# An audio tower's third group moved forward, and the experts' second layer in three 16-bit products

## What is computed

```
interp  = cubic_interpolate_1d(x, 4x);  windows of 64
kw      = 0.5*(w+1.3)^2 + 0.5*exp(-0.5*(w-0.7)^2)
M       = |fft(kw)|;  tok = softmin(M*sigmoid(M-0.12*max), 0.9*max)
x1      = layernorm(tok)
attn    = sigmoid(q k^T * 8) v, 8 heads;  h = tok + relu(attn @ Wo)
x2      = layernorm(h)
shared  = relu(relu(x2 @ sW1) @ sW2) @ sW3
experts = relu(relu(x2 @ eW1[e]) @ eW2[e]) @ eW3[e],  e = 0..3
gated   = the two experts with the largest gates, weighed
out     = h + shared + gated
```

## Time and profile before

| what | us |
|---|---|
| three runs, median (lowest, highest) | 170.97 (167.11, 171.64) |
| profiled execution, its own time | 166.02 |
| its span | 164.2 |
| TensorE matmul busy | 151.4 (92%) |
| ScalarE busy | 113.2 (69%) |
| VectorE busy | 108.6 (66%) |
| GpSimd busy | 54.5 (33%) |

### The profile page before, as it was taken

How to read it: one execution, slowest core, us unless ns; L and a number is a source line. 1 busy time by engine, 2 the same in 40 slices (tenths; PEclk the granted TensorE clock), 3 DMA queues, 4 the chain that set the end, 5 groups by cost and what they waited for, 6 DMA issues and landing times.

```text
span 164.2 us, 6647 instructions
## 1 busy us (share of the span) xinstructions
PE 151.4 (92%) x2824; PEld 91.4 (56%) x2824; DVE 108.6 (66%) x277; ACT 113.2 (69%) x155; POOL 54.5 (33%) x101
## 2 busy tenths in 40 slices
PE   7998695999979999999899999999999999999970
PEld 2488533545446576666657454634756665676760
DVE  2497998989766767776583949776469775454421
ACT  3598972978859898989695989467444827548310
POOL 4000019685896673645235171717000000000000
PEclk9999569999999999999999999999999999999999
DMA  4380000174796676747576000000010100101101
GB/s 110 99 251 0 4 0 0 64 188 112 174 233 197 188 217 173 213 128 227 160 218 173 13 4 4 4 0 0 4 33 4 33 19 16 35 4 31 34 21 43
DMA packets 13182, 14.09 MB, mean 86 GB/s; under 512 B 1241, under 2 KB 12413, under 8 KB 13089
## 3 DMA queue, kind: packets, MB, share of 16 engines
q1 hardware_dynamic: 12864, 13.47, 29.6%
q10 hardware_dynamic: 288, 0.20, 0.4%
HBM read 9.06 MB, written 4.60 MB: 83 GB/s over the span
## 4 chain that ended last, share of the span: by engine, by line
PE 69%; DVE 10%; ACT 7%; DMA 5%; POOL 4%; issue 2%; DVEq 0%; POOLq 0%; ACTq 0%
PE ps L456 14%; PE ps L438 12%; PE ps L558 8%; PE ps L576 7%; PE ps L615 7%; PE ps L467 4%; PE ps L585 3%; DMA y_stage<-YP 3%; DMA YS<-y_stage 2%; PE ps L600 2%; PE ps L317 2%; PE ps L306 2%; PE ps L479 1%; PE ps L492 1%; POOL norm L1262 1%
## 5 line engine op out<-in xcount | busy, mean ns | idle before, releaser
L1169 ACT ACTIVATE probs<-ps 125x1000 f32<-125x1000 f32 x64 | 61.9, 1008 | 11.1 <-PE ps L438 8.7
L456 PE MATMUL ps<-probs,xn 124*32 124x250 f32 (+1 forms) x512 | 39.2, 376 | 0.0
L438 PE MATMUL ps<-YS,XT 128*32 128x500 f16 x448 | 34.2, 376 | 1.6 <-DMA YS<-y_stage 1.5
L456 PEld LDWEIGHTS ps<-probs,xn 124*32 124x32 f32 (+1 forms) x512 | 15.7, 109 | 12.5 <-issue 2.4
L1196 ACT ACTIVATE H2r<-ps,wf 128x500 f32<-128x500 f32 x16 | 10.8, 676 | 15.4 <-PE ps L576 15.4
L838 DVE COPY ZS<-ps 128x250 f32<-128x250 f32 x32 | 12.9, 412 | 9.9 <-PE ps L456 9.8
L1042 DVE TENSOR_TENSOR area<-H2r,ps 128x500 f32<-128x500 f32 x16 | 10.8, 673 | 10.1 <-ACT H2r L1196 8.6
L576 PE MATMUL ps<-area,wf 128*64 128x500 f32 x64 | 16.7, 585 | 0.0
L1183 ACT ACTIVATE area<-ps,wf 128x500 f32<-128x500 f32 x24 | 15.9, 672 | 0.9 <-PE ps L558 0.9
L438 PEld LDWEIGHTS ps<-YS,XT 128*32 128x32 f16 x448 | 10.7, 96 | 9.9 <-ACT probs L1169 4.0
L819 DVE CAST YP<-ps 128x500 f16<-128x500 f32 x14 | 9.5, 677 | 8.5 <-PE ps L397 8.5
(11 more groups left out here) (157 smaller groups left out, 258.2 us busy)
## 6 DMA issues: line engine op xcount, KB each, us to landing
YS<-y_stage SPq DMA_DIRECT2D x40, 125.0 KB, 3.1
y_stage<-YP SPq DMA_DIRECT2D x10, 250.0 KB, 2.8
YS<-y_stage SPq DMA_DIRECT2D x8, 250.0 KB, 3.9
y_stage<-YP SPq DMA_DIRECT2D x8, 125.0 KB, 4.1
tower_out<-res SPq DMA_DIRECT2D x8, 124.0 KB
wf<-wf_in SPq DMA_DIRECT2D x1, 648.0 KB, 5.9
wa<-wa_in SPq DMA_DIRECT2D x1, 512.0 KB, 5.1
ch<-ch_in SPq DMA_DIRECT2D x1, 160.0 KB, 4.9
```

The source lines that it names most:

```text
L438: last = mm(ps[k0:k1, 2 * (n % 2) + j, 0:TG].rearrange("p (h n) -> p h n", h=2), XT[:, g % 3, (2 * bb + cj) * P + k0:(2 * bb + cj) * P + k ...
L456: last = mm(ps[R * hh:R * hh + R, 4 + bb, half * TB:(half + 1) * TB], xn[0:keys, 4 * g + 2 * bb + cj, :], probs[0:keys, n % 3, hh, :], sta ...
L1169: fn(probs[:, n % 3].rearrange("p (j h) n -> p j (h n)", j=2), ps[0:P, 2 * (n % 2):2 * (n % 2) + 2, 0:TG], ACT.Sigmoid, scale=SCORE_SCALE) ...
```

## The change

**Third group a step sooner.** TensorE does x_transpose(2) at step 4 and y_project(2,·) at steps 5 and 6, each one step earlier, with the transpose in bank 6 in place of 7. VectorE does total and variance of `third` before part_low(4), takes x_take(2) before the total of `later`, y_take(2,0) before z_take(0,1), and centre(later) after y_take(2,1). GpSimd computes the token of `later` after the square of `third`. SyncE sends group 2's first half before it reads back group 1's second.

**The second layer of experts.** For groups 1 to 7, layer2(g,0) and layer2(g,1) are three 16-bit products: high weight x high activation, low weight x high, high weight x low. Group 0 keeps the 32-bit product. GpSimd splits the weights into w2p. ScalarE now does relu1 for all four experts. The high part is a cast, `high1(g,e)`, on VectorE; for expert 3 of groups 1 to 4 on ScalarE. The low part is a subtraction on GpSimd, `low1(g,e)`, in order of g and e, behind norm2(7) in its program. H1 now has one buffer, and relu1(g,e) waits for low1 of the group before; the parts lie in H1p, over YS, with two buffers.

The diff, cut to its core:

```diff
+        def high_on_act(g, e):
+            return e == E - 1 and g <= NG // 2
...
-            for k in range(2):
-                send(1, k)
-                read_back(1, k)
+            send(1, 0)
+            read_back(1, 0)
+            send(1, 1)
             send(2, 0)
+            read_back(1, 1)
             send(2, 1)
             read_back(2, 0)
...
-                if n == 5:
+                if n == 4:
                     x_transpose(2)
-                if n in (6, 7):
-                    y_project(2, n - 6)
+                if n in (5, 6):
+                    y_project(2, n - 5)
...
             y_take(1, 0)
-            part_low(4)
             dve.wait_ge(square_pool, 1)
             total(third, masked)
             variance(third)
+            part_low(4)
...
             y_rest(1, 1)
+            x_take(2)
             dve.wait_ge(token_pool, 1)
             total(later, tok)
+            y_take(2, 0)
+            z_take(0, 1)
+            y_take(2, 1)
             centre(later)
-            x_take(2)
-            z_take(0, 1)
-            y_take(2, 0)
-            y_take(2, 1)
             z_take(0, 2)
...
+                    if g == 1 and k == 0:
+                        pe.wait_ge(w2_split, 2)
+                    pe.wait_ge(h1_lo, E * (g - 1) + 2 * k + 2)
+                    for i, (w, h) in enumerate(((0, 0), (1, 0), (0, 1))):
+                        for j in range(2):
+                            e = 2 * k + j
+                            last = mm(ps[F * j:F * j + F, 3 + k, 0:TG], w2p[:, w, e * F:(e + 1) * F],
+                                      H1p[:, g % 2, h, e, :], start=(i == 0), stop=(i == 2))
...
+            def high1(g, e):
+                if high_on_act(g, e):
+                    return
+                dve.wait_ge(l1_act, E * g + e + 1)
+                if g >= 3:
+                    dve.wait_ge(l2_mm, 3 * (g - 2) + e // 2 + 1)
+                v.tensor_copy(H1p[:, g % 2, 0, e, :], H1[:, e, :]).then_inc(h1_hi, 1)
...
                 if g < NG:
                     weigh(g, 0)
+                if g + 1 < NG:
+                    high1(g + 1, 0)
...
                 if g + 1 < NG:
-                    relu1(g + 1, 3)
+                    high1(g + 1, 2)
+                    high1(g + 1, 3)
...
+                if g == 1:
+                    act.wait_ge(l2_mm, e // 2 + 1)
                 if g >= 2:
-                    act.wait_ge(l2_mm, 3 * (g - 1))
+                    act.wait_ge(h1_lo, E * (g - 2) + e + 1)
...
                     if g + 1 < NG:
                         relu1(g + 1, k)
+                    if g + 1 < NG and k == 2:
+                        relu1(g + 1, 3)
+                        if high_on_act(g + 1, 3):
+                            high1(g + 1, 3)
...
             norm2(NG - 1)
+
+            def low1(g, e):
+                if high_on_act(g, e):
+                    pool.wait_ge(h1_hi_act, g)
+                else:
+                    pool.wait_ge(h1_hi, high_count(g, e))
+                if g >= 3:
+                    pool.wait_ge(l2_mm, 3 * (g - 2) + e // 2 + 1)
+                v.tensor_tensor(H1p[:, g % 2, 1, e, :], H1[:, e, :], H1p[:, g % 2, 0, e, :],
+                                ALU.subtract).then_inc(h1_lo, 1)
+
+            for g in range(1, NG):
+                for e in range(E):
+                    low1(g, e)
```

More of the change, by code:

```diff
@@ L222, in build, with high_count, x_bank @@
         unit_of = [(bb, half) for half in range(2) for bb in range(2)]
+        def high_on_act(g, e):
+            return e == E - 1 and g <= NG // 2
+        def high_count(g, e):
+            return sum(1 for n in range(1, g + 1) for i in range(E if n < g else e + 1) if not high_on_act(n, i))
+        def x_bank(g):
+            return {0: 1, 2: 6}.get(g, 7)
         def y_bank(g, k):
@@ L375, in x_transpose @@
                     pe.wait_ge(x2t_cp, g - 4)
-                xt = half_bank(7 if g else 1, 128, 4)
+                xt = half_bank(x_bank(g), 128, 4)
                 for i in range(4):
@@ L570, in layer2 @@
                 if k < 2:
-                    pe.wait_ge(l1_act, 3 * g + (2, 3)[k])
-                    if k == 1:
-                        pe.wait_ge(l1_dve, 2 * g + 1)
-                    for j in range(2):
-                        e = 2 * k + j
-                        last = mm(ps[F * j:F * j + F, 3 + k, 0:TG],
-                                  wf[:, WF["w2"][0] + e * F:WF["w2"][0] + (e + 1) * F], H1[:, g % 2, e, :],
-                                  start=True, stop=True)
+                    if g == 0:
+                        pe.wait_ge(l1_act, 2 * k + 2)
+                        for j in range(2):
+                            e = 2 * k + j
+                            last = mm(ps[F * j:F * j + F, 3 + k, 0:TG],
+                                      wf[:, WF["w2"][0] + e * F:WF["w2"][0] + (e + 1) * F], H1[:, e, :],
+                                      start=True, stop=True)
+                        last.then_inc(l2_mm, 1)
+                        return
[3 more added lines that the diff above has]
+                    for i, (w, h) in enumerate(((0, 0), (1, 0), (0, 1))):
+                        for j in range(2):
+                            e = 2 * k + j
+                            last = mm(ps[F * j:F * j + F, 3 + k, 0:TG], w2p[:, w, e * F:(e + 1) * F],
+                                      H1p[:, g % 2, h, e, :], start=(i == 0), stop=(i == 2))
                 else:
                     pe.wait_ge(l2_act, 3 * g + 2)
-                    pe.wait_ge(l1_dve, 2 * g + 2)
+                    pe.wait_ge(l1_dve, g + 1)
                     for m in range(2):
@@ L1025, in _, with relu_shared @@
             gate_rows(0)
-            def relu1(g, e):
-                n = (E + 1) * g + e
+            def relu_shared(g):
+                n = (E + 1) * g + E
                 dve.wait_ge(l1_mm, n + 1)
@@ L1050, in finish @@
                                 h2[:, 4 * g:4 * g + 4, :], ALU.add).then_inc(res_done, 1)
-            for e in range(3, E + 1):
-                relu1(0, e)
+            relu_shared(0)
             routing_take(0)
@@ L1068, in _ @@
                     weigh(g, 1)
+                if g + 1 < NG:
+                    high1(g + 1, 1)
                 if g == 0:
@@ L1084, in _ @@
                 if g + 1 < NG:
-                    relu1(g + 1, 4)
+                    relu_shared(g + 1)
                 if g == 2:
@@ L1197, in relu2 @@
                    bias=wf[:, WF["b2"][0] + k:WF["b2"][0] + k + 1]).then_inc(l2_act, 1)
-            for e in range(3):
+            for e in range(E):
                 relu1(0, e)
@@ L1286, in _ @@
             square_rows(third)
+            pool.wait_ge(act1, 6)
+            v.tensor_tensor(tok[:, later, 0:NBIN], masked[:, later, :], dist[:, later, :],
+                            ALU.subtract).then_inc(token_pool, 1)
             inverse_deviation(slice(8, 12), third)
```

46 lines of the change are left out of this document (27 added, 19 removed).

## The result

The changed kernel takes 184.28 us (median of 6 runs, 182.73 to 184.88), the kernel before, in the same session, 166.10 (median of 6, 164.62 to 171.64). The ratio is 1.117, with a 95% interval of 1.111 to 1.122. Each ratio here leaves out executions that a disturbed clock set apart, so it can differ a little from the ratio of the medians. The change makes the kernel 18.2 us slower, where +9.7 was forecast. The direction was right and the time lies in the range, but the size was about half of what came.

A forecast was written before the change was run, and what follows sets the result against it. TensorE's queue was taken to bound a group of the last stage. Terms of 6.0 + 1.5 + 2.0 + 0.2 gave +9.7 us on a middle of 169.04, so 178.7 us (+5.7%), range 170.5 to 187.

The forecast's parts named there:

- The main wait: TensorE before layer2(1,0): waits for two GpSimd subtractions behind norm2(7), starting at about 117.8 instead of 111.84, +6.0 us.
- term 3: Feed-forward groups: a new chain of relu, cast and subtractions outweighs TensorE's shorter 16-bit matmuls, +2.0 us in sum.
- term 4: The head: the scores' DMA wait goes, but later VectorE and GpSimd work delays projections, net +0.2 us.
- Term 1: Start of layer2(1,0): it now waits for GpSimd's low1(1,0) and low1(1,1) behind norm2(7), +6.0 us (bounds 4.5 and 7).
- Term 2: After the wait before layer2(1,0): TensorE's clock falls to half speed for some 6 us, +1.5 us (bounds 0 and 3).
- the cast waits for the subtraction: Groups 5 to 7: expert 3's cast on VectorE waits until low1(g,2) ends, +1.4 us more, 180.1 us; chance 0.15.
- The 0.5 for `part_low(4)`: Head: total(third) ahead of part_low(4) on VectorE, for which y_part(5) waits, makes the scores lose 0.5 us.
- The other two waits: Head: y_project(3,0) waits for x_take(3), 0.8 us more than the 0.5; y_project(4,1) is about 0.65 us late.

The follow-up runs named there:

- e3_first2: The changed kernel with group 1's second layer in 32 bits too, so that the split begins with group 2: 177.71 us, ratio 1.078.
- e5_stub_sub: The kernel before with 28 GpSimd subtractions of 128x500 added, into a buffer nobody reads and that nobody waits for: 172.95 us, ratio 1.046.

## Why the prediction was half right

The main wait and its cause came as forecast. What failed is term 3 and, far less, term 4: without group 1 they were put at 1.65 + 0.2 = +1.85 and came out at 11.5. That the time of 184.28 still lies in the range is in part luck. The range was laid around a middle of 169.04 for the kernel before, which then measured 166.10. Counted as a loss, its upper end is 187 - 169.04 = +18.0, and +18.2 came.

- **Term 1, +6.0: right.** 5.8 was measured by the starts, 5.88 by the wait, 6.0 by leaving it out (14.89 to 8.85 in `e3_first2`). The chain came as worked out: the subtraction 1.14 (forecast 1.15), the cast 0.40 (0.41).
- **Term 2, +1.5: the mechanism right, a bit large.** The clock fell. Group 1, which holds this term and the +0.35 of term 3, lost 0.97 in all. It came back after some 3 us of work, not 6. What the term lacked is the second fall, behind the gate's wait; it is part of group 4's loss below.
- **Term 3, +2.0: this is the step that failed.** Of it 0.35 was for group 1, so +1.65 for the others, and these measured about 10.1: group 2 +0.63 (forecast 0), group 3 +5.86 (+0.3), group 4 +1.23 (+0.05), groups 5 and 6 +1.30 (+0.6), the end +1.07 (+0.7). The failing sentence is that of group 2, "the gate's matmuls in the queue and its arithmetic on VectorE and ScalarE set its pace in both: 0", and +0.3 for group 3 beside it. The gate's arithmetic does set the pace there, and for that reason nothing that slows it is free. I asked what TensorE would wait for and priced the new work on GpSimd; I didn't ask what GpSimd's reading does to VectorE's own instructions. Group 4's loss, too, comes from there: it is the clock after the gate's wait of 3.68.
- **The rival "the cast waits for the subtraction" came true in its mechanism,** at a chance of 0.15. It said 5.2 us from layer2(g,2) to layer2(g+1,1); it is 165.46 - 160.27 = 5.19. I had it at +1.4 and for the casts of groups 5 to 7 alone. The hold of the two-input instructions in groups 2 and 3 stood in no rival. With this 1.4 and the 3.65 of `e5_stub_sub`, a number that only the runs gave, the forecast would have been near +14.8.
- **Term 4, +0.2: too small.** It measured +1.38 in the profiles of before and after, 2.0 between the means of four and five traces, and +1.5% (2.4 us) with the head alone. The 0.5 for `part_low(4)` became a wait of 1.47, half of it because `total(third)` was itself held (0.89 in place of 0.17) by GpSimd's subtraction, which the change had moved beside it. The other two waits, for `x_take(3)` and for the projections of group 4, came where they were expected, of 1.03 and 0.94.

The row that speaks for the hold was in the trace of before, and I had not looked for it:

```profile
99.77 0.19 DVE L904 TENSOR_TENSOR gt<-gt 125x32 f32<-125x32 f32 x1
99.94 0.61 POOL L1242 TENSOR_TENSOR lnsq<-ln 125x256 f32<-125x256 f32 x1 [2.10 <-DVE ln L855]
99.99 0.61 DVE L906 TENSOR_TENSOR gt<-gt 125x32 f32<-125x32 f32 x1
```

Two instructions of one size, 0.2 us apart: 0.19, and 0.61 beside GpSimd's square, ending with it. A group by shape whose mean (400 ns for L906) is twice that of its neighbours is where to look.
